# Two products of the delta rule in one of 128 columns, and the query products moved behind the solves

## The chip, the cores and the metric

The kernel runs on one core of a Trainium2 chip. The metric is the device time of one execution in microseconds (us), median of several. The engines are named as the profile names them: PE is the matrix engine (PEld its weight loads), DVE the vector engine, ACT the scalar engine, POOL the GpSimd engine, SP the engine that issues DMAs.

## What is computed

The program is a decoder of two layers over 4 batches of 512 tokens with 128 channels. Each layer has an attention, a cross attention and a feed forward part, with a layer norm after each. The change lies in the attention of the second layer, a delta rule with 16 heads of 64 channels. Cut to what matters, it is:

```python
Q = (x @ Wq).reshape(B, T, H, D)
K = (x @ Wk).reshape(B, T, H, D)
V = (x @ Wv).reshape(B, T, H, D)
beta = jax.nn.sigmoid(x @ Wbeta + b_beta)
K = K / jnp.maximum(jnp.linalg.norm(K, axis=-1, keepdims=True), EPS)
def step(W, inp):
    q_t, k_t, v_t, b_t = inp
    pred = jnp.einsum('bhij,bhj->bhi', W, k_t)
    err = v_t - pred
    W_new = W + b_t[..., None, None] * jnp.einsum('bhi,bhj->bhij', err, k_t)
    o_t = jnp.einsum('bhij,bhj->bhi', W_new, q_t)
    return (W_new, o_t)
W0 = jnp.zeros((B, H, D, D), dtype=x.dtype)
_, O = lax.scan(step, W0, xs)
out = jnp.moveaxis(O, 0, 1).reshape(B, T, H * D)
return out @ Wout
```

## The kernel before

The recurrence is not run token by token. The 512 tokens of a batch are cut into 8 chunks of 64, and 4 heads of one batch make a unit, so that there are 16 units (`u`; `m = u // 2` counts pairs of units, `j = u % 2` the half in the pair). Per unit two things are done.

The preparation, `d_prep_tensor`, `d_prep_scalar` and `d_prep_vector`, works on all chunks of a unit at once. It makes the values (`values`), the queries (`queries`), finishes a block inverse (`corner`, `fold`), multiplies it into the values and keys side by side (`solve`, four times, the result copied by ACT to `d_UW`), and multiplies keys with queries (`products`); DVE masks these into `d_PT`. From `d_UW` four products follow, all fp32 with a 64x64 operand: the transitions (`"da"`, 24 matmuls of 64 columns, `d_UW` times keys), the steps (`"db"`, 28), the reads (`"dr"`, 28, `d_UW` times `d_PT`) and the outputs (`"do"`, 32). DVE turns the transitions into `d_AT` (`d_id` minus the product, line 2001, four instructions) and subtracts the reads from the queries in `d_QT` (line 2013, two instructions). ACT copies the steps to `d_S` and the outputs to `d_OT`.

The chain, `d_chain_tensor` and `d_chain_vector`, runs over the chunks in order: for chunks 1 to 7 a product of `d_S` with `d_AT`, one of `d_S` with `d_QT`, and on DVE an addition to `d_S` (line 2065). After chunk 3 and after chunk 7 DVE adds the finished half to `d_OT` (line 2070). PE then waits for `d_ot`, the second of these additions, and multiplies `d_OT` with the output weights (`d_wo`, 8 matmuls).

`d_order` weaves, per `u`, the chain of unit `u` with the preparation of unit `u + 1`, and with more: in odd `u` up to 9 `d_rows_*` makes the keys of a later pair (its DVE part scales them at line 1675, after a row of small instructions on `d_z`, `d_za`, `d_zb`, `d_zy`, `d_sb` and `d_f`); in even `u` from 2 to 10 `d_turn_*` transposes them (line 1598), multiplies each chunk with itself from `d_KT`, and DVE masks that into `d_L` (line 1687). At the end, from `u` = 13 on, the cross attention (`e_*`) and the start of the feed forward part (`f_*`) are woven in. Each engine runs its instructions in the order in which the woven generators issue them; every `yield` is a place where another generator may be served, and the numbers beside a generator are its share.

Products of these stages take turns in a ring of 5 PSUM banks, `ringD`: whoever takes a bank first waits until its last content has been read, by the semaphore and value that were given when it was taken.

In this stage PE works on quarters of the array. `TILES` sets the order of the matmuls so that four in a row use four different quarters; `solve` takes two of the quarters in turn. One fp32 matmul shows in the trace as two loads and two matmul records.

```python
TILES = [(p, c, half, par) for p in range(2) for c in range(4) for half, par in ((0, 0), (1, 1), (0, 1), (1, 0))]
```

## Time and profile before

| | |
|---|---|
| median of three runs | 1605.43 us (1594.52, 1605.43, 1605.57) |
| the profiled execution | 1597.89 us |
| its span | 1596.1 us |
| PE busy | 1451.0 us, 91% of the span |
| DVE busy | 1125.7 us, 71% |
| ACT busy | 925.6 us, 58% |
| the delta rule's woven stage | from about 1000 to about 1440 us of the span |

The profile gives for every engine what it did and when, how long it sat idle, and what released it. The chain of work that ended last is followed back from the last instruction, each step to what released it. "issue" is time in which an engine waited for nothing that the profile shows.

### The profile page before, as it was taken

The page shows a single profiled execution, that of the slowest core. Times are in us where ns is not written, and L with a number is a line of the kernel's source. Part 1 is how long each engine was busy: PE and PEld are TensorE (multiplying, and loading weights), DVE is VectorE, ACT ScalarE, POOL GpSimd, SP SyncE. Part 2 cuts the span into 40 slices and gives each one's busy share as a digit, 9 for nine tenths or more (in the row PEclk, how much of TensorE's full clock was granted, in tenths as well). Part 3 has the DMA queues.
Part 4 walks back from the last instruction along what each step waited for, and adds up shares of the span by engine and source line. Part 5 has one row for each costly group of instructions (what it writes and reads, how often), then busy time and mean ns, then how long its engine had stood idle before and what let it go on. Part 6 is the DMA issues. An engine that isn't in the chain of part 4 may idle for free.

```text
span 1596.1 us, 44182 instructions
## 1 busy us (share of the span) xinstructions
PE 1451.0 (91%) x19224; PEld 800.5 (50%) x19224; DVE 1125.7 (71%) x2297; ACT 925.6 (58%) x1301; POOL 694.8 (44%) x741
## 2 busy tenths in 40 slices
PE   8888888899999999999988988999999989999996
PEld 4222222343434334333434544787877778775453
DVE  6778877888877885867727668576777765574654
ACT  2788775787867876887672443555455544342220
POOL 2111131566655665676580108457776567010000
PEclk9999999999999999999999999999999999989898
DMA  4000003333322341332302000000000002000000
GB/s 166 1 1 1 1 1 108 106 95 91 95 77 77 91 109 52 104 91 78 94 6 79 1 1 14 16 17 17 4 17 17 17 3 67 28 2 1 8 7 14
DMA packets 32417, 70.80 MB, mean 44 GB/s; under 512 B 5328, under 2 KB 7056, under 8 KB 31968
## 3 DMA queue, kind: packets, MB, share of 16 engines
q1 hardware_dynamic: 32224, 67.98, 14.5%
q8 instruction: 151, 2.47, 0.7%
q14 instruction: 42, 0.34, 0.1%
HBM read 47.45 MB, written 20.51 MB: 43 GB/s over the span
## 4 chain that ended last, share of the span: by engine, by line
PE 62%; ACT 14%; DVE 14%; issue 7%; POOL 2%; DMA 0%; ACTq 0%; DVEq 0%; SPq 0%; POOLq 0%
PE ps L160 60%; ACT b_X L961 3%; ACT a_E L470 3%; DVE b_mx L899 2%; ACT b_EH L169 2%; POOL b_EL L979 1%; DVE a_MX L433 1%; PE ps L242 1%; ACT b_Hk L169 1%; PE ps L1598 1%; DVE b_Lk L840 1%; ACT b_OT L169 1%; DVE X L234 1%; DVE st L172 1%; DVE b_rd L1072 1%
## 5 line engine op out<-in xcount | busy, mean ns | idle before, releaser
L979 POOL TENSOR_TENSOR b_EL<-b_X,b_EH 128x1024 f16<-128x1024 f32 x160 | 341.1, 2132 | 193.5 <-ACT b_EH L169 193.3
L961 ACT ACTIVATE b_X<-ps 128x1024 f32<-128x1024 f32 x160 | 163.7, 1023 | 88.6 <-PE ps L160 86.8
L1784 POOL TENSOR_TENSOR d_tmp<-d_G,d_XI 128x31 f32<-128x31 f32 (+15 forms) x248 | 126.5, 510 | 162.6 <-DVE d_G L1713 143.7
L433 DVE TENSOR_REDUCE a_MX<-ps 128x2 f16<-128x1024 f32 x128 | 155.3, 1227 | 45.7 <-PE ps L160 45.3
L169 ACT ACTIVATE b_EH<-b_X 128x1024 f16<-128x1024 f32 x160 | 169.1, 1057 | 26.0 <-PE ps L160 14.8
L899 DVE TENSOR_REDUCE b_mx<-ps 128x2 f32<-128x1024 f32 x128 | 155.9, 1218 | 37.0 <-PE ps L160 35.1
L160 PE MATMUL ps<-b_M,b_S 128*64 128x512 f16 (+1 forms) x1408 | 175.6, 381 | 3.4 <-ACT b_X L961 3.3
L470 ACT ACTIVATE a_E<-ps 128x1024 f32<-128x1024 f32 x128 | 131.1, 1024 | 49.2 <-PE ps L160 49.0
L1787 POOL TENSOR_TENSOR d_XI<-d_XI,d_tmp 128x31 f32<-128x31 f32 (+15 forms) x248 | 139.6, 563 | 19.4
L160 PEld LDWEIGHTS ps<-b_M,b_S 128*64 128x64 f16 (+1 forms) x1408 | 70.9, 108 | 80.3 <-ACT b_X L961 14.1
L452 POOL TENSOR_TENSOR a_QS<-a_QS,a_MR 128x512 f16<-128x512 f16 x16 | 18.5, 1156 | 201.0 <-ACT a_MR L169 197.1
L2526 POOL TENSOR_TENSOR f_Y<-X,f_bo 128x512 f32<-128x512 f32 x4 | 6.0, 1496 | 188.8 <-DVE X L234 106.9
L160 PE MATMUL ps<-f_XM,f_Wh 128*128 128x512 f16 x256 | 78.2, 388 | 0.0
L160 PE MATMUL ps<-b_Hk,b_Hq 64*128 64x154 f16 (+1 forms) x512 | 66.8, 309 | 12.4 <-DVE b_mx L899 9.9
L160 PE MATMUL ps<-a_E,a_VA 128*32 128x512 f32 x512 | 69.5, 615 | 1.4
L160 PE MATMUL ps<-b_EH,b_VH 128*64 128x512 f16 x320 | 64.7, 400 | 4.2 <-ACT b_OT L169 2.1
L160 PEld LDWEIGHTS ps<-b_Hk,b_Hq 64*128 64x128 f16 x512 | 19.8, 93 | 95.2 <-issue 48.1
L160 PE MATMUL ps<-d_KV,d_XE 64*64 64x128 f32 x1024 | 65.4, 273 | 0.5 <-ACT d_XE L169 0.3
L169 ACT ACTIVATE d_UW<-ps 128x512 f32<-128x512 f32 x64 | 38.2, 597 | 46.3 <-PE ps L160 46.3
L1389 ACT ACTIVATE c_SG<-ps 128x512 f32<-128x512 f32 x36 | 21.5, 597 | 74.1 <-PE ps L160 70.7
L160 PE MATMUL ps<-a_QS,a_KS 32*128 32x512 f16 x256 | 50.0, 387 | 14.8 <-ACT a_E L470 14.3
L2065 DVE TENSOR_TENSOR d_S<-d_S,ps 128x128 f32<-128x128 f32 x96 | 26.9, 280 | 49.5 <-PE ps L160 48.9
(323 smaller groups left out, 3322.3 us busy)
## 6 DMA issues: line engine op xcount, KB each, us to landing
b_S<-s_xk SPq DMA_DIRECT2D x48, 336.0 KB, 6.3
b_M<-s_xq SPq DMA_DIRECT2D x48, 256.0 KB, 5.0
s_xk<-b_Hk SPq DMA_DIRECT2D x16, 336.0 KB, 2.2
s_xk<-b_Lk SPq DMA_DIRECT2D x16, 336.0 KB, 2.5
s_xq<-b_Hq SPq DMA_DIRECT2D x16, 256.0 KB, 2.0
s_xq<-b_Lq SPq DMA_DIRECT2D x16, 256.0 KB, 2.0
d_XI<-eye SPq DMA_DIRECT2D x8, 512.0 KB, 3.8
f_w<-f_w SPq DMA_DIRECT2D x1, 2048.0 KB, 8.7
```

The lines of the kernel that those rows point to most:

```text
L160: return e.matmul(out, lhsT, rhs, start=start, stop=stop, skip_group_check=True)
L169: return e.activation(out, a, ACT.Copy)
L433: v.e.tensor_reduce(out, PS[:, bk:bk + 2, :], AX, ALU.max).then_inc(sem("a_mx"), 1)
L452: p.e.tensor_tensor(a_QS[G % 4], a_QS[G % 4], a_MR[G % 2], ALU.add).then_inc(sem("a_q2"), 1)
L470: a.e.activation(a_E[c][:, 2 * hp:2 * hp + 2, :], PS[:, bk:bk + 2, :], ACT.Exp, scale=float(D) ** -0.5).then_inc(sem("a_ex"), 1)
L899: last = v.e.tensor_reduce(b_mx[:, 0, :, n], PS[:, bk:bk + 2, :], AX, ALU.max)
L961: a.e.activation(b_X[k % 2], PS[:, bk:bk + 2, :], ACT.Exp, scale=0.125).then_inc(sem("b_ex"), 1)
L979: last = p.e.tensor_tensor(b_EL[k % 6], b_X[k % 2], b_EH[k % 6], ALU.subtract)
L1389: a.e.activation(c_SG[n % 3], PS[:, bank["cgu", b, p], :], ACT.Silu).then_inc(sem("c_sl"), 1)
L1784: e.tensor_tensor(tm, a, x, ALU.mult).then_inc(*p.step())
L1787: last = e.tensor_tensor(z, z, tm, ALU.subtract)
L2065: e.tensor_tensor(s, s, PS[:, 6, o:o + 128], ALU.add).then_inc(sem("d_s"), 1)
```

## The change

The masked query products no longer have a tile `d_PT` of their own. DVE writes them over the values, in the half of `d_KV` that lies beside the keys, once the four solves of the unit have read the values (`d_um`). The transitions and the reads then have the same stationary operand `d_UW` and moving operands that lie side by side, so a new function `spread` makes them as one product: per half of the unit (`p`) 12 matmuls of 128 columns and 2 of 64. DVE takes the results apart with eight instructions instead of six, `d_AT` and `d_QT` in turn. The query products move on PE from ahead of the solves to behind them, and the steps come ahead of `spread`. The core of the diff:

```diff
-            def transitions(r, p, c, par):
-                return U[r, at_chunk(p, c, par), 64:128], keys_of(r, p, c, par)
-
-            def reads(r, p, c, par):
-                i = at_chunk(p, c, par)
-                return U[r, i, 64:128], P[r, i, :]
+            def spread(p):
+
+                bk = [ringD.take(t, ("dr", u, p, half), 1, "d_qq", 4 * u + 2 * p + half + 1) for half in range(2)]
+                t.wait_ge("d_u", 4 * u + 4)
+                t.wait_ge("d_pt", 2 * u + 2)
+                for k, c, half, par in TILES:
+                    if k == p and 2 * c + half > 0:
+                        r, n = HALF[half], 2 if 2 * c + half < 7 else 1
+                        last = mm(e, PS[HALF[par], bk[half], 128 * c:128 * c + 64 * n], U[r, at_chunk(p, c, par), 64:128],
+                                  KV[r, c, 0:n, 4 * j + head(p, par), :])
+                last.then_inc(sem("d_rm"), 1)
...
-            products()
             yield
             for k in range(4):
                 solve(k)
                 yield
-            yield
-            update("da", "d_a", "d_am", 64, 128, 1, 6, transitions)
+            products()
             yield
             update("db", "d_b", "d_bm", 64, 128, 0, 6, steps)
             yield
-            yield
-            t.wait_ge("d_pt", 2 * u + 2)
-            update("dr", "d_qq", "d_rm", 256, 64, 1, 7, reads)
+            for p in range(2):
+                spread(p)
+                yield
             yield
             update("do", "d_o", "d_om", 256, 64, 0, 7, outputs)
...
             v.wait_ge("d_ptm", u + 1)
+            v.wait_ge("d_um", 4 * u + 4)
             for par in range(2):
-                e.tensor_tensor(d_PT[:, 8 * par:8 * par + 8, :], PS[:, bank["dp", u, par], :].rearrange("p (i n) -> p i n", i=8),
-                                d_mu.unsqueeze(1).broadcast_to([128, 8, 64]), ALU.mult).then_inc(sem("d_pt"), 1)
-                yield
...
+                e.tensor_tensor(KV[:, :, 0, 4 * j + par:4 * j + 4:2, :].rearrange("p c a n -> p a c n"),
+                                PS[:, bank["dp", u, par], :].rearrange("p (a c n) -> p a c n", a=2, c=4),
+                                d_mu.unsqueeze(1).unsqueeze(1).broadcast_to([128, 2, 4, 64]), ALU.mult).then_inc(sem("d_pt"), 1)
+                yield
+            A = d_AT[j].rearrange("p (c k) a n -> p c k a n", k=2)
             q = d_QT[j].rearrange("p a (c k n) -> p a c k n", c=4, k=2)
+            for p in range(2):
+                v.wait_ge("d_rm", 2 * u + p + 1)
+                for half in range(2):
+                    o = 1 - half
+                    ps = PS[:, bank["dr", u, p, half], :].rearrange("p (c k n) -> p c k n", c=4, k=2)
+                    e.tensor_tensor(A[:, o:o + 3, half, p, :], d_id.unsqueeze(1).broadcast_to([128, 3, 64]), ps[:, o:o + 3, 1],
+                                    ALU.subtract).then_inc(sem("d_a"), 1)
+                    x = q[:, p, o:4, half, :]
+                    e.tensor_tensor(x, x, ps[:, o:4, 0], ALU.subtract).then_inc(sem("d_qq"), 1)
+                yield
...
-                    streams.append((later(9, split(lane)), 18))
+                    streams.append((later(13, split(lane)), 22))
```

PE in a loop with an odd `u` (the preparation of a unit whose keys lie in `d_KV_192`), from the middle of the solves to the outputs, before:

```order
L160 MATMUL ps<-d_KV_192,d_XE 64x128 x16
L160 MATMUL ps<-d_S_217,d_AT_201 64x64 x4
L160 MATMUL ps<-d_QT_211,d_S_217 64x64 x4
L160 MATMUL ps<-d_KV_192,d_XE 64x128 x8
L160 MATMUL ps<-d_S_217,d_AT_201 64x64 x4
L160 MATMUL ps<-d_QT_211,d_S_217 64x64 x4
L160 MATMUL ps<-d_KV_192,d_UW 64x64 x24
L160 MATMUL ps<-d_UW,d_KV_192 64x64 x28
L160 MATMUL ps<-d_QT_211,d_S_217 64x64 x4
L160 MATMUL ps<-d_PT,d_UW 64x64 x60
```

The solves are the rows with `d_XE`, the chain the rows with `d_S`; `d_KV_192,d_UW` are the 24 transitions, `d_UW,d_KV_192` the 28 steps, `d_PT,d_UW` the 28 reads and the 32 outputs. The same place after the change:

```order
L160 MATMUL ps<-d_KV_192,d_XE 64x128 x8
L160 MATMUL ps<-d_QT_210,d_KT_194 64x64 x32
L160 MATMUL ps<-d_S_217,d_AT_201 64x64 x4
L160 MATMUL ps<-d_QT_211,d_S_217 64x64 x4
L160 MATMUL ps<-d_UW,d_KV_192 64x64 x28
L160 MATMUL ps<-d_KV_192,d_UW 64x128 x11
L160 MATMUL ps<-d_KV_192,d_UW 64x64
L160 MATMUL ps<-d_KV_192,d_UW 64x128
L160 MATMUL ps<-d_KV_192,d_UW 64x64
L160 MATMUL ps<-d_QT_211,d_S_217 64x64 x4
```

The query products (`d_QT,d_KT`) now stand behind the last solve, the steps are the first to need `d_UW`, and `spread` has the chain's last product between its two halves; the other half and the outputs follow.

DVE in the same kind of loop, from the last small steps ahead of the key scaling to the second addition to `d_OT`, before:

```order
L2065 TENSOR_TENSOR d_S_217<-d_S_217,ps 128x128
L1668 TENSOR_TENSOR d_sb<-d_z,d_zy 128x32
L1670 TENSOR_TENSOR d_f<-d_zy,d_sb 128x32
L2001 TENSOR_TENSOR d_AT_200<-d_id,ps 128x3x64 x4
L1675 TENSOR_TENSOR d_KV_192<-d_KV_192,d_f 128x512
L2070 TENSOR_TENSOR d_OT_219<-d_OT_219,ps 128x2x256
L1675 TENSOR_TENSOR d_KV_192<-d_KV_192,d_f 128x512 x2
L2013 TENSOR_TENSOR d_QT_210<-d_QT_210,ps 128x2x3x64
L2013 TENSOR_TENSOR d_QT_210<-d_QT_210,ps 128x8x64
```

And after the change, up to the same addition:

```order
L1668 TENSOR_TENSOR d_sb<-d_z,d_zy 128x32
L1670 TENSOR_TENSOR d_f<-d_zy,d_sb 128x32
L2002 TENSOR_TENSOR d_AT_200<-d_id,ps 128x3x64
L2005 TENSOR_TENSOR d_QT_210<-d_QT_210,ps 128x3x64
L2002 TENSOR_TENSOR d_AT_200<-d_id,ps 128x3x64
L2005 TENSOR_TENSOR d_QT_210<-d_QT_210,ps 128x4x64
L1675 TENSOR_TENSOR d_KV_192<-d_KV_192,d_f 128x512
L2002 TENSOR_TENSOR d_AT_200<-d_id,ps 128x3x64
L2005 TENSOR_TENSOR d_QT_210<-d_QT_210,ps 128x3x64
L2002 TENSOR_TENSOR d_AT_200<-d_id,ps 128x3x64
L2005 TENSOR_TENSOR d_QT_210<-d_QT_210,ps 128x4x64
L2063 TENSOR_TENSOR d_OT_219<-d_OT_219,ps 128x2x256
```

The addition to `d_OT`, for which the output product on PE waits, stood ahead of both subtractions from `d_QT`; it now stands behind all eight instructions that take `spread` apart, in this loop and in every other one.

## Rows read from the trace of the kernel before

**Rows 1.** The page: span; busy time and instructions; the queue of instruction transfers (packets, MB).

```profile
span 1596.1 us, 44182 instructions
...
PE 1451.0 (91%) x19224; PEld 800.5 (50%) x19224; DVE 1125.7 (71%) x2297; ACT 925.6 (58%) x1301; POOL 694.8 (44%) x741
...
q8 instruction: 151, 2.47, 0.7%
```

**Rows 2.** Windows: stretch, its length, then busy us (instructions) of PE, PEld, DVE, ACT, POOL; granted clock.

```profile
1117.05:1132.93 15.88, 14.25 (x572) 13.21 (x571) 13.79 (x32) 7.40 (x13) 14.23 (x22) 1.00 0.02 4
1137.59:1159.14 21.55, 18.75 (x717) 17.11 (x717) 13.40 (x40) 10.35 (x17) 10.89 (x24) 1.00 0.02 4
```

**Rows 3.** Chain that ended last, 1116 to 1160 us: start, us, what.

```profile
1126.85 0.61 ACT d_UW L169
...
1131.14 1.29 issue
...
1157.01 1.56 issue
...
1159.14 0.59 PE ps L242 x4
```

**Rows 4.** Timeline of PEld from 1126 us, loop u = 3: start, us, instructions, [idle before].

```profile
1126.53 0.37 PEld L160 LDWEIGHTS ps<-d_S,d_AT 64*64 64x64 f32 x8
...
1127.56 0.83 PEld L160 LDWEIGHTS ps<-d_KV,d_UW 64*64 64x64 f32 x48 [0.43 <-issue]
1128.26 1.05 PEld L160 LDWEIGHTS ps<-d_UW,d_KV 64*64 64x64 f32 x55
...
1129.46 1.53 PEld L160 LDWEIGHTS ps<-d_PT,d_UW 64*64 64x64 f32 x93
1132.42 0.44 PEld L160 LDWEIGHTS ps<-d_PT,d_UW 64*64 64x64 f32 x24 [1.43 <-issue]
1132.93 1.19 PEld L160 LDWEIGHTS ps<-d_wo,d_OT 128*128 128x128 f32 x10
```

**Rows 5.** Timeline of PEld from 1145 us, loop u = 4: last solve, first `d_KT` product.

```profile
1146.24 0.85 PEld L160 LDWEIGHTS ps<-d_KV,d_XE 64*64 64x64 f32 x16
...
1149.65 1.05 PEld L160 LDWEIGHTS ps<-d_KT 64*64 64x64 f32 x64 [1.09 <-ACT d_UW L169]
```

**Rows 6.** DMA from 1118 to 1158 us, 40 slices of 1 us: GB/s by packet start; totals.

```profile
GB/s 16 0 0 0 16 0 0 16 0 0 0 16 0 0 0 16 0 0 0 0 0 16 0 0 16 0 0 0 16 0 0 0 0 0 16 0 0 16 0 0
DMA packets 10, 0.16 MB, mean 4 GB/s; under 512 B 0, under 2 KB 0, under 8 KB 0
```

**Rows 7.** Timeline 1078 to 1108 us: loads for 32 and for 128 columns.

```profile
1087.54 1.09 PEld L160 LDWEIGHTS ps<-d_XE,d_L 32*32 32x32 f32 x64 [0.21 <-issue]
...
1093.98 1.73 PEld L160 LDWEIGHTS ps<-d_KV,d_XE 64*64 64x64 f32 x32
```

**Rows 8.** Timeline of DVE from 1120 us, loop u = 3.

```profile
1122.46 0.69 DVE L1990 TENSOR_TENSOR d_PT<-ps,d_mu 128x512 f32<-128x512 f32 x1
...
1126.86 0.66 DVE L172 SCALAR_TENSOR_TENSOR d_zy<-d_zb,d_zy 128x64 f32<-128x64 f32 x1
...
1127.63 0.60 DVE L1668 TENSOR_TENSOR d_sb<-d_z,d_zy 128x32 f32<-128x32 f32 x1
...
1128.58 1.15 DVE L2001 TENSOR_TENSOR d_AT<-d_id,ps 128x192 f32<-128x192 f32 x4
1129.64 0.68 DVE L1675 TENSOR_TENSOR d_KV<-d_KV,d_f 128x512 f32<-128x512 f32 x1
1130.25 0.68 DVE L2070 TENSOR_TENSOR d_OT<-d_OT,ps 128x512 f32<-128x512 f32 x1
...
1132.58 1.14 DVE L2013 TENSOR_TENSOR d_QT<-d_QT,ps 128x384 f32<-128x384 f32 x2
```

**Rows 9.** DVE groups by shape from 1000 to 1480 us: the mask into `d_L`.

```profile
L1687 DVE TENSOR_TENSOR d_L<-ps,d_ml 128x512 f32<-128x512 f32 x26 | 16.7, 684 | 24.5 <-PE ps L160 24.5
```

**Rows 10.** Chain that ended last, 1412 to 1427 us, shares by line.

```profile
by line: DVE f_XM L2468 30.8%; PE ps L160 21.8%; DVE f_Wl L172 16.1%; DVE X L234 6.9%; DVE e_Qp L2300 5.0%; DVE st L172 4.6%; issue 4.2%; ACT f_mk L169 4.1%; DVE d_AT L2001 3.6%; DVE d_S L2065 2.7%; DVE st L181 1.2%; DVE st L187 1.2%; DVE s
```

More of the change, by code:

```diff
@@ L1797, in d_prep_tensor @@
             KV, KT, L, X = d_KV[m % 3], d_KT[m % 2], d_L[m % 2], d_XE[u % 2]
-            Q, P, U, x = d_QT[j], d_PT, d_UW, d_XS[b % 2]
+            Q, U, x = d_QT[j], d_UW, d_XS[b % 2]
             def values(k):
@@ L1944, in d_prep_scalar @@
                 yield
-            yield
-            yield
             a.wait_ge("d_bm", u + 1)
@@ L1992, in d_prep_vector @@
                 yield
-            for _ in range(4):
-                yield
-            v.wait_ge("d_am", u + 1)
-            A = d_AT[j].rearrange("p (c k) a n -> p c k (a n)", k=2)
-            for half in range(2):
-                o = 1 - half
-                ps = PS[:, bank["da", u, half], 128 * o:128 * o + 384]
-                for a in range(2):
-                    last = e.tensor_tensor(A[:, o:o + 3, half, 64 * a:64 * a + 64], d_id.unsqueeze(1).broadcast_to([128, 3, 64]),
-                                           ps.rearrange("p (c a n) -> p c a n", c=3, a=2)[:, :, a], ALU.subtract)
-                last.then_inc(sem("d_a"), 1)
@@ L2004, in d_prep_vector @@
-            yield
-            yield
-            yield
-            v.wait_ge("d_rm", u + 1)
-            q = d_QT[j].rearrange("p a (c k n) -> p a c k n", c=4, k=2)
-            for half in range(2):
-                o = 1 - half
-                x = q[:, :, o:4, half, :]
-                ps = PS[:, bank["dr", u, half], :].rearrange("p (a c n) -> p a c n", a=2, c=4)
-                e.tensor_tensor(x, x, ps[:, :, o:4], ALU.subtract).then_inc(sem("d_qq"), 1)
-            yield
-            yield
+            A = d_AT[j].rearrange("p (c k) a n -> p c k a n", k=2)
@@ L2019, in d_chain_tensor @@
+            for _ in range(3):
+                yield
         def d_chain_tensor(t, u):
```

14 lines of the change are left out of this document (6 added, 8 removed).

## Prediction

> **What bounds the kernel now.** I read the page first: PE is busy 1451 of 1596.1 us [rows 1]. Then the windows of two loops of the stage. In the one that scales keys (u = 3) PE is busy 14.25 of 15.88 us, but DVE is busy 13.79 as well; in the one that transposes keys (u = 4) PE has 18.75 of 21.55 us and DVE 13.40 [rows 2]. So PE sets the pace in both, and in the first DVE is only just behind it. What PE loses between its instructions stands in the chain of work that ended last, over the same two loops [rows 3]. There are three kinds of loss:
>
> - It waits for the last copy to `d_UW` before the transitions. The last solve ends at 1126.53 and the chain's two products then take 0.47 us; the transitions start at 1127.56 [rows 4]. About 0.6 us, with the copy itself in the chain.
> - It waits with nothing to wait for, "issue": 1.29 us at 1131.14 and 1.56 us at 1157.01 [rows 3], each inside the long row of small products with `d_PT` [rows 4].
> - In the transposing loops it waits 1.09 us for the copies ahead of the first `d_KT` product [rows 5].
>
> The "issue" waits are the arrival of PE's own instructions, as I read the DMA rows. Queue q8 moves 151 packets, 2.47 MB; PE and PEld together have 38,448 instructions [rows 1], so 64 bytes each and about 255 to a packet. In the dense stretch the packets start 3 to 4 us apart: slices 0, 4, 7, 11, 15 and again 21, 24, 28 [rows 6]. The window of u = 3 holds 1143 instructions in 15.88 us, 4.5 packets; that of u = 4 holds 1434, 5.6 packets in 21.55 us [rows 2]. Both give 3.5 to 3.85 us for a packet. A row of small products uses one up in 128 x 15 ns = 1.9 us, and then runs dry.
>
> **The change, part by part.** The reference time is the profiled execution, 1597.89 us, span 1596.1; the median of three is 1605.43. I make the sum against the mean of all four, 1600.9 us, since one execution lies 11 us below the others.
>
> *The product itself.* A matmul of 64 columns shows as two loads. 48 of them take 0.70 us from the first to the start of the next group [rows 4], so a matmul costs 0.029 us; transitions and reads cost 52 x 0.029 = 1.52 us. The trace has no 128 columns over four quarters. It has them over two: 32 loads in 1.73 us, 0.054 us each, 0.108 per matmul [rows 7]. Bounds for one of the 24 new matmuls are 0.029 (the columns cost nothing) and 0.108 us (four quarters help no more than two). I take half the upper one, 0.054, because the solves' price is that of streaming columns and four quarters share it twice as far. That gives 24 x 0.054 + 4 x 0.029 = 1.41 us, a gain of 0.1 us per unit. The bounds give a gain of 0.7 and a loss of 1.2 us.
>
> The row of 32-column products weighs in here: 64 loads in 1.09 us [rows 7], 16 ns each, no cheaper than 64 columns at 15 ns. The Trainium skill (TensorEngine Tiling (Array Packing), Instruction Overhead) says that a matmul has some 60 cycles of overhead, so that one column costs as much as 60; the trace agrees that narrower is no cheaper, though 15 ns at 2.4 GHz is 36 cycles. By that rule 128 columns cost twice 64, and the merge would give PE nothing; the sum would be 16 x 0.1 = 1.6 us less.
>
> *Instructions.* 24 matmuls fewer are 96 instructions, 0.375 packet: 1.4 us per unit, wherever the packets set the pace.
>
> *Query products behind the solves.* Their 32 matmuls, 64 x 15 ns = 1.0 us, are only moved. They now cover the last copy to `d_UW`, 0.6 us, and in the five transposing loops they stand between transposes and the first `d_KT` product and cover its 1.09 us.
>
> *The masks.* Before, the masks ran under the solves and nobody waited. Now the first `spread` needs both. I count from the end of the last solve, with the times of [rows 4, 8]. In a loop with key rows (odd u, 1 to 9): the query products end at 1.05. DVE: mask 1.25 to 1.9, a `d_zy` step 0.66, second mask to 3.2. PE has had chain and steps since 2.4 and waits 0.8. `spread` runs to 4.0. DVE meanwhile adds `d_S`, and makes `d_sb` and `d_f`, until 4.3. Then four instructions that take the first half apart: `d_AT` costs 1.15 / 4 = 0.29 and `d_QT` 1.14 us for both, so 0.29 + 0.29 + 0.29 + 0.36 = 1.2 us, to 5.5. A key scaling of 0.7, to 6.2; the second half, to 7.4; and only then the addition to `d_OT`, 0.6, to 8.0.
>
> *What is late next.* The output product on PE waits for that addition. Before, it was over at 1130.93 and the output product started at 1132.93 [rows 4, 8], 2 us later, 6.4 us after the last solve. Now PE is through with the outputs at about 5.2 (halves of `spread`, a bank released by the first `d_QT`, outputs 1.0 us) and stands until 8.0. Behind the waiting output product stand the next unit's values and queries, and so DVE and ACT. Taking off the 1.05 us of query products that moved in here, it is 6.95 us against 6.4: a loss of 0.55 us, in five loops 2.8 us. The "issue" wait and the copy wait are gone, but the wait for `d_OT` is as long as both and more.
>
> *Transposing loops* (even u, 2 to 10). Before, 1147.1 to 1159.14 us, 12.0 us, of which 1.09, 1.56 and about 0.6 us are waits [rows 3, 5], so 8.8 us of work. After, 8.8 + 1.0 - 0.1 = 9.7 us to the end of the outputs, the first half of `spread` ending 2 us earlier, at 7.8. The masks are long done. DVE: first half to 9.0, then two masks into `d_L`, 1.4 us [rows 9], which now stand between the halves, to 10.5; second half to 11.7; `d_OT` at 12.4. Less 1.0 is 11.4, against 12.0, or 12.6 where a transpose of `X` stands ahead. I take a gain of 0.9, in five loops 4.5 us.
>
> *Loops without either* (u = 0, 11, 12, 13). Masks at 2.6, first half of `spread` to 3.4, DVE to 4.7, 5.9, `d_OT` at 6.5; less 1.05 is 5.5 against 6.4. Gain 0.9, in four 3.6 us; I take 3.2, since the last two are mixed with other work.
>
> *Last preparation* (u = 14). Here DVE is on the chain itself, with `f_XM` at 30.8% and `f_Wl` at 16.1% [rows 10]. Both masks now stand behind these and `spread` waits for them, two more instructions are added, and `e_Qp` stands behind the first half. A loss of 0.5 to 2.5, I take 1.5 us. Moving `f_Wl` back by four steps makes this no worse.
>
> *The first unit* has free room; 0.3 us for the covered copy.
>
> Sum: -2.8 + 4.5 + 3.2 - 1.5 + 0.3 = 3.7, so 4 us. 1600.9 - 4 = 1597 us.
>
> **The rivals.**
>
> *The packets still decide, and the wait for `d_OT` is hidden.* If DVE runs well ahead and its addition comes by the end of the outputs, each unit is worth what its instructions are: 1.3 us in eight loops, 2.0 in five transposing ones (96 instructions, and the 1.09 us in part), 20 us, less 1.5: 1582 us. For it: packets 3 to 4 us apart. Against it: DVE has 13.79 of 15.88 us in one kind of loop [rows 2], and its order is fixed, addition last. Chance 0.28, 1573 to 1588.
>
> *Everything goes at once*, the refill waits with it, and 30 us are won: 1571 us and below. It needs DVE to be no bound at all. Chance 0.04.
>
> *Slower: the addition to `d_OT` comes later than I count.* One mechanism, DVE's tail in front of the output product. If each of its eight pieces costs 0.12 us more, because a piece of 192 elements does not overlap the one before as the four in a row did, the tail grows by 1 us in 15 units: 4 - 15 = -11, 1612 us. It decides from 0.27 us per unit on, the 4 us spread over 15 units; so a small error of mine turns the sign. Chance 0.22, 1601 to 1620.
>
> *As forecast*, 1588 to 1601: 0.46.
>
> **How the numbers follow.** A measurement of this kernel can tell about 1% from no change, 16 us. Faster by more: 0.04, and two thirds of 0.28, with a little of the middle case, 0.24. Slower by more: the top third of 0.22, 0.08. Within: 0.68. The range 1580 to 1612 leaves out the fastest case, the faster third of the packet case and the top of the slower one, 0.04 + 0.10 + 0.05. The likeliest case alone has 1588 to 1601.
>
> **What the profile after would show.** PE waits ahead of the output product for DVE's `d_OT`, 1 to 3 us in nearly every unit: if this row is missing, my main step is wrong and the time is near 1582. A new wait of PE for the mask in `d_KV`, 0.3 to 0.8 us, in loops without transposes. The waits for `d_UW` ahead of the steps are gone, and the 1.09 us in front of `d_KT` products. "issue" waits above 0.5 us are fewer than one per unit. Loads with 128 columns are 27 ns apart (54 would mean that four quarters share nothing). q8 has 6 packets fewer, 145. The forecast fails if the eight pieces on DVE cost other than 1.2 us per half, or if the spacing of packets is not a limit but follows from PE's pace.

## The result, and the profile after

| | before | after |
|---|---|---|
| median | 1605.43 us (1594.52 to 1608.83, 5 runs) | 1652.38 us (1642.87 to 1655.02, 5 runs) |
| profiled execution | 1597.89 us, span 1596.1 | 1642.87 us, span 1640.7 |
| PE busy | 1451.0 us, 91% | 1456.9 us, 89% |
| start of the output product in loop u = 0, and in u = 15 | 1057.5, 1471.8 | 1062.1, 1518.9 |

The change is 2.85% slower: ratio 1.0285, 95% interval 1.0246 to 1.0324. I had forecast 1597 us, range 1580 to 1612; the time lies 40 us above the range. The page of the changed kernel, against [rows 1]:

```profile
PE 1456.9 (89%) x18456; PEld 808.8 (49%) x18456; DVE 1126.7 (69%) x2329; ACT 926.8 (56%) x1301; POOL 695.6 (42%) x741
...
q8 instruction: 145, 2.38, 0.6%
```

PE has 768 matmul records fewer and six instruction packets fewer, as the diff says, and yet stands idle longer. The place is certain: between the output products of u = 0 and u = 15 lie 414.3 us before and 456.8 after, 42.5 of the 44.6 us by which the spans differ. By kind of loop: the five that transpose keys (u = 2 to 10, even) are 25.6 us longer, the five that scale keys (odd u to 9) 9.5, the last five 7.4. Every kind lost, where I had expected a gain in the transposing loops and in most of the last ones. The output product of u = 0 itself starts 4.6 us later, although the last group ahead of the stage starts 2.0 us earlier (997.87 against 999.82 us): another 6.6 us are lost in the first preparation and loop u = 0. Of the kernels below, those that have only the query products moved, or moved as in the change, lose 6 to 8 us there, those with the products ahead of the solves at most 2, so this is the move's. (`three` and `four`, where `queries` is moved as well, lose 2 to 4.) After the last output product the changed kernel is 2.4 us shorter, which no edit explains.

Part of the loss goes with PE's clock. The trace shows it granted in full (2.4 GHz) or at half (1.2 GHz). Between the output products of u = 0 and u = 15 it is at half for 13.7 us before and for 30.7 us after, most of the latter in u = 2, 6, 8 and 13, where the kernel before has none. From execution to execution the time follows it as well: over 94 executions of the kernel before, the mean granted clock lies between 0.972 and 0.986, and the time falls by 1.4 us for each 0.001 more. The five executions of the changed kernel have a mean of 0.974, those before 0.979; by that slope, and this is an estimate, some 8 of the 47 us go with the lower clock. No run changes the clock alone, so whether it falls because PE waits more is not shown.

PE's waits in the changed kernel, from 1000 to 1520 us (who waits, for what; us in total, times, longest):

```profile
PE ps L160 <- DVE d_L L1687: 10.1, 5, 2.4
PE ps L160 <- ACT d_KT L169: 9.6, 5, 2.3
PE ps L160 <- DVE d_OT L2063: 8.4, 8, 1.8
PE ps L160 <- issue: 8.2, 13, 0.9
PE ps L1598 <- ACT d_UW L169: 6.4, 5, 1.3
PE ps L242 <- DVE X L234: 6.4, 4, 2.3
PE ps L160 <- DVE d_KV L1991: 5.4, 8, 2.8
PE ps L160 <- ACT d_XE L169: 5.2, 6, 1.4
```

The same view of the kernel before, for PE:

```profile
PE ps L160 <- issue: 20.0, 19, 1.8
PE ps L160 <- ACT d_KT L169: 4.4, 5, 0.9
PE ps L160 <- ACT d_UW L169: 4.3, 10, 1.1
```

The 20 us without a releaser have fallen to 8, and further than the row says: eight of its 13 waits, 0.71 us each, stand ahead of the first solve of a unit and end 0.1 us after ACT's copy to `d_XE`. They belong to that copy, which makes its row 10.9 us and leaves 2.5 us of waits for instructions. But six waits for other engines are new and the one for `d_KT` has doubled, and only two of them (for `d_OT` and for the mask in `d_KV`) are in my prediction. Those for `d_L`, for `d_KT` and for `d_UW` ahead of the transposes belong to loops that transpose. This is one of them, u = 4, PEld first, then ACT and DVE (start, us, instructions, idle before and releaser; where a row of PEld says "issue", the list above names the releaser of PE's wait):

```profile
1160.94 0.71 PEld L160 LDWEIGHTS ps<-d_KV,d_XE 64*64 64x64 f32 x12
...
1162.85 1.02 PEld L160 LDWEIGHTS ps<-d_QT,d_KT 64*64 64x64 f32 x64 [0.17 <-issue]
1165.30 0.42 PEld L1598 LDWEIGHTS ps<-ident,d_KV 128*128 128x128 f32 x4 [1.42 <-ACT d_UW L169]
...
1170.79 1.05 PEld L160 LDWEIGHTS ps<-d_KT 64*64 64x64 f32 x64 [1.76 <-issue]
...
1174.82 1.81 PEld L160 LDWEIGHTS ps<-d_KV,d_UW 64*64 64x64 f32 x92 [1.98 <-issue]
1178.82 0.42 PEld L242 LDWEIGHTS ps<-ident,X 128*128 128x128 f32 x4 [2.19 <-issue]
1179.21 0.97 PEld L160 LDWEIGHTS ps<-d_wo,d_OT 128*128 128x128 f32 x8
```

```profile
1164.16 0.60 ACT L169 ACTIVATE d_KT<-ps 128x512 f32<-128x512 f32 x1 [2.97 <-PE ps L160]
1164.65 0.59 ACT L169 ACTIVATE d_UW<-ps 128x512 f32<-128x512 f32 x1
...
1169.21 0.98 ACT L169 ACTIVATE d_S<-ps 128x512 f32<-128x512 f32 x2 [2.62 <-PE ps L160]
1170.08 0.60 ACT L169 ACTIVATE d_KT<-ps 128x512 f32<-128x512 f32 x1
```

```profile
1173.62 0.41 DVE L2005 TENSOR_TENSOR d_QT<-d_QT,ps 128x256 f32<-128x256 f32 x1
...
1174.02 1.28 DVE L1687 TENSOR_TENSOR d_L<-ps,d_ml 128x512 f32<-128x512 f32 x2
```

ACT's first copy to `d_KT` may only run when the query products of this unit have read the tile it overwrites (`d_ptm`, in `d_turn_scalar`). Before, those products stood ahead of the solves and were long through. Now they start at 1162.85, behind two groups of transposes; ACT stands 2.97 us, and its fourth copy to `d_UW`, whose product was ready, stands behind it. PE's third group of transposes needs the ring bank which that copy frees, and waits 1.42 us. Next, the last `d_KT` copy stands on ACT behind the two to `d_S`: 1.76 us. Then the second half of `spread` needs banks that hold the `d_L` products, and DVE masks these only after it has taken the first half apart: 1.98 us. Last, the transposes of `X` wait for DVE's line 234, which stands behind the second half and the addition to `d_OT`: 2.19 us.

In loops that scale keys the picture is that of the prediction, and one wait more. Loop u = 3, PEld, then DVE:

```profile
1135.62 0.88 PEld L160 LDWEIGHTS ps<-d_KV,d_XE 64*64 64x64 f32 x16 [0.87 <-issue]
...
1139.17 0.88 PEld L160 LDWEIGHTS ps<-d_KV,d_XE 64*64 64x64 f32 x16
...
1142.85 0.77 PEld L160 LDWEIGHTS ps<-d_KV,d_UW 64*64 64x64 f32 x26 [0.40 <-DVE d_KV L1991]
...
1147.49 1.64 PEld L160 LDWEIGHTS ps<-d_wo,d_OT 128*128 128x128 f32 x14 [1.80 <-DVE d_OT L2063]
```

```profile
1143.91 0.35 DVE L2002 TENSOR_TENSOR d_AT<-d_id,ps 128x192 f32<-128x192 f32 x1 [0.34 <-PE ps L160]
...
1144.71 0.41 DVE L2005 TENSOR_TENSOR d_QT<-d_QT,ps 128x256 f32<-128x256 f32 x1
...
1146.77 0.68 DVE L2063 TENSOR_TENSOR d_OT<-d_OT,ps 128x512 f32<-128x512 f32 x1
```

The wait of 0.87 us ahead of the first solve is the one I had missed. `fold` is copied by ACT to the block inverse (`d_mt`, the releaser `d_XE` of the list above), and the query products used to stand between `fold` and the first solve and cover that copy.

### The profile page after: what moved, and what is told of

Its sections match the earlier page's. It is cut to its first block, busy times and chain, and to the rows that moved or that the text cites. A ratio compares the mean times of both kernels' runs of the same rounds, so it can differ in the third digit from the quotient of the medians.

```text
span 1640.7 us, 42711 instructions
## 1 busy us (share of the span) xinstructions
PE 1456.9 (89%) x18456; PEld 808.8 (49%) x18456; DVE 1126.7 (69%) x2329; ACT 926.8 (56%) x1301; POOL 695.6 (42%) x741
## 4 chain that ended last, share of the span: by engine, by line
PE 60%; DVE 17%; ACT 15%; issue 6%; POOL 1%; DMA 0%; ACTq 0%; DVEq 0%; SPq 0%; POOLq 0%
PE ps L160 57%; ACT b_X L961 3%; ACT a_E L470 3%; DVE b_mx L899 2%; ACT b_EH L169 1%; POOL b_EL L979 1%; DVE a_MX L433 1%; PE ps L242 1%; ACT b_Hk L169 1%; DVE d_QT L2005 1%; DVE X L234 1%; PE ps L1598 1%; DVE d_AT L2002 1%; DVE b_Lk L840 1%; DVE d_KV L1991 1%
## 5 line engine op out<-in xcount | busy, mean ns | idle before, releaser
L169 ACT ACTIVATE b_EH<-b_X 128x1024 f16<-128x1024 f32 x160 | 169.1, 1057 | 25.9 <-PE ps L160 14.7
L160 PE MATMUL ps<-d_KV,d_XE 64*64 64x128 f32 x1024 | 69.4, 281 | 10.9 <-issue 5.7
L160 PE MATMUL ps<-b_Hk,b_Hq 64*128 64x154 f16 (+1 forms) x512 | 66.8, 309 | 12.9 <-DVE b_mx L899 10.4
L2058 DVE TENSOR_TENSOR d_S<-d_S,ps 128x128 f32<-128x128 f32 x96 | 27.0, 281 | 66.8 <-PE ps L160 66.3
L160 PE MATMUL ps<-d_KV,d_UW 64*64 64x64 f32 (+1 forms) x1920 | 55.7, 263 | 18.1 <-DVE d_L L1687 10.1
L160 PEld LDWEIGHTS ps<-d_KV,d_XE 64*64 64x64 f32 x1024 | 59.8, 140 | 13.8 <-issue 13.8
```

Source lines behind the costliest of these rows:

```text
L160: return e.matmul(out, lhsT, rhs, start=start, stop=stop, skip_group_check=True)
L169: return e.activation(out, a, ACT.Copy)
L2058: e.tensor_tensor(s, s, PS[:, 6, o:o + 128], ALU.add).then_inc(sem("d_s"), 1)
```

## The experiments

Ratios are against the kernel before on the same chip, with the 95% interval. The kernel before has medians of 1601.5 to 1605.4 us on the chips used, so a difference in us between two kernels that did not run on the same chip is uncertain by some 4 us, and by more where the intervals are wide. The theories: **order**, that the query products lost the work they covered and put ACT's queue out of step; **tail**, that DVE's eight pieces stand in front of what PE needs (`d_OT`, banks); **packets**, that fewer PE instructions are worth 1.3 us per unit.

**The two parts apart.** First the move without the merge, and the merged product without the move, its masks one by one behind the solves that free them:

```diff
 # move_alone, against the kernel before (units 0 to 13)
-            products()
             yield
             for k in range(4):
                 solve(k)
                 yield
+            products()
...
 # merge_alone, against the changed kernel (units 0 to 13)
+            products()
             yield
             for k in range(4):
                 solve(k)
                 yield
-            products()
...
-            v.wait_ge("d_um", 4 * u + 4)
             for par in range(2):
+                v.wait_ge("d_um", 4 * u + 2 * par + 2)
```

> The kernel before, with the query products behind the four solves in units 0 to 13 (units 14 and 15 as before), the masks into d_PT four steps later on DVE; transitions, reads and their take-apart unchanged. Order theory (the place of the query products carries the loss of 47 us): the waits of the changed kernel come back without the merge. About 0.95 us ahead of the first solve for ACT's copy d_mt, 12 us in all, and 3 to 5 us in each of the five transposing loops, because the copies to d_KT stand on ACT behind a wait for the query products; I expect 1605 + 30 = 1635 us, 1622 to 1650. Tail theory (DVE's eight pieces and the addition to d_OT behind them carry it): the move alone only covers waits, 1605 or a little less, 1592 to 1608. My prediction's count for the move was a gain of 10 us.

Measured: 1633.93 us, 1.0196 (1.0116 to 1.0276). The move alone costs 32 us, where the change has 47, and the order theory's two waits show in it, that of the transposes and the missed one ahead of the first solve. They are not all of it: "issue" is 33.1 us here, against 20.0 before, 5.7 of it ahead of the first solves as above. The other 27.4 are waits for instructions inside rows of small products, 7 us more than before; the moved products now stand in one row with the steps and transitions. And the mean granted clock is 0.974.

```profile
PE ps L160 <- issue: 33.1, 31, 2.1
PE ps L1598 <- ACT d_UW L169: 6.4, 5, 1.3
PE ps L160 <- ACT d_XE L169: 5.2, 6, 1.4
```

> The changed kernel, with the query products back ahead of the solves in units 0 to 13 and each mask on DVE placed behind the two solves that read its half of the values (d_um at 4u + 2 and 4u + 4); spread and the eight pieces on DVE stay. Order theory: the waits ahead of the first solve (12.6 us in the changed kernel) and most of those in the transposing loops go; left are the tail and the d_UW wait; 1652 - 35 = 1617 us, 1605 to 1628. Tail theory: most of the loss stays, 1640 to 1655, since the addition to d_OT still stands behind the eight pieces.

Measured: 1654.58 us, 1.0313 (1.0235 to 1.0391). A miss, and the price I gave to the order theory was wrong here. PE's waits say why this kernel isn't the clean half that I took it for:

```profile
PE ps L160 <- ACT d_KT L169: 14.0, 10, 2.3
PE ps L160 <- DVE d_S L2067: 11.4, 22, 1.7
PE ps L160 <- DVE d_L L1687: 10.1, 5, 2.4
PE ps L160 <- DVE d_OT L2072: 9.2, 9, 1.8
```

The wait for `d_XE` is gone, but DVE now stands in its queue at masks that wait for solves, and the chain's additions to `d_S` behind them are late 22 times. The waits for `d_L` and `d_OT` are those of the changed kernel, so they come with the merge.

So a cleaner one: query products ahead of the solves and masked into `d_PT` just as before, and a `spread` whose moving operand is one access pattern from the keys across to `d_PT`, two rows of 64 words a fixed distance apart.

```diff
+                        if 2 * c + half < 7:
+                            k0 = KV_AT[m % 3] + 1024 * c + 512 + 64 * (4 * j + head(p, par))
+                            k1 = 35492 - 9508 + 64 * i
+                            x = d_both[r, k0:k0 + 64]
+                            x = bass.AP(x.tensor, x.offset, [list(x.ap[0]), [k1 - k0, 2], [1, 64]])
+                            last = mm(e, PS[HALF[par], bk[half], 128 * c:128 * c + 128], U[r, i, 64:128], x)
```

> The merge without anything else: the kernel before, with transitions and reads as one product of 128 columns (spread, two halves, eight pieces on DVE), but the query products stay ahead of the solves and are masked into d_PT as before, under the solves. The moving operand is one access pattern that reaches from the keys to d_PT. Sum theory: the loss of the whole change (47 to 51 us) is that of the move (32 us, measured) and that of the merge, so the merge costs 15 to 19 us: 1618 us (1612 to 1624), with waits for d_L, 10 us, and d_OT, 9 us, in the trace and PE's issue waits down from 20 to under 10 us. Rival, my prediction's: the merge is worth the 96 instructions of a unit, 1.3 us in 13 loops, less the tail: 1590 to 1603. Second rival: the time of the kernel with the masks per parity (1654.6) is the merge's own and not that of its masks: 1640 to 1655.

Measured: 1635.92 us, 1.0191 (1.0134 to 1.0247). The merge by itself costs 33 us, twice the sum theory's price, in none of the three forecasts' ranges and far from my prediction's gain. Move and merge together make 65 us where the change has 47, so their losses overlap. By kind of loop, in the profiled executions, the overlap is 5 us in the transposing loops (9.1 and 21.8 us alone, 25.6 together) and 11 in those that scale keys (11.2 and 9.7 alone, 9.5 together). One part shows: the 27.4 us of waits for instructions that the move has alone are 2.5 us in the changed kernel. The rest was not tried. PE's waits in this kernel:

```profile
PE ps L160 <- ACT d_KT L169: 15.5, 12, 2.3
PE ps L160 <- DVE d_L L1690: 10.2, 5, 2.4
PE ps L160 <- DVE d_OT L2071: 9.8, 9, 2.1
PE ps L160 <- issue: 8.2, 10, 1.5
```

**Repairs of order in the changed kernel.** Each takes one of the waits away and leaves the work as it is.

```diff
 # turn_later
-                    streams.append((later(18, turn(lane, m)), 30.59))
+                    streams.append((later(21, turn(lane, m)), 33.59))
...
 # ot_first: steps between the two halves of the take-apart, not behind them
                 yield
-            for _ in range(3):
-                yield
+                if p == 0:
+                    for _ in range(2):
+                        yield
```

> The changed kernel, with the transposes of the keys and what follows them three steps later in the five transposing loops, so that PE has issued the query products before the first transpose and ACT's copy to d_UW no longer stands behind a copy to d_KT that waits for them. The five loops are 25.7 us longer than before in the changed kernel. Order theory: the waits of 1.3 to 1.6 us behind the fourth d_UW copy in five loops go, and the second d_KT product no longer waits for a copy behind the two of d_S: 7 to 15 us less, 1642 us (1636 to 1647). Tail theory: the masks into d_L only come later, in front of the addition to d_OT; no gain or 5 us worse, 1650 to 1658.

Measured: 1641.36 us, 1.0245 (1.0168 to 1.0323), 11 us less by the medians, 6 by the ratios, whose intervals overlap with the changed kernel's. The profiled executions are clearer: the five transposing loops are 12.9 us longer than before instead of 25.6; the other kinds change by 1.5 us or less.

> The changed kernel, with two more steps between the two halves of the take-apart on DVE, so that in the loops where it fits (10 of 16) the second addition to d_OT stands between the halves and no longer behind all eight pieces. Tail theory, step 'what is late next' of my prediction: PE's wait ahead of the output product falls by the 1.2 us of a half in ten loops, 8 to 12 us less, 1642 us. Order theory: the waits that the trace shows for d_OT are 10.7 us over eight loops, of which some comes back as a wait of the next chain for d_AT and d_QT: 2 to 8 us less, 1647 us. If the tail carried most of the loss, over 20 us would have to go.

Measured: 1638.99 us, 1.022 (1.0143 to 1.0296), 13 us less by the medians, 10 by the ratios. That is the tail theory's number, and more than I gave it by the waits. But it isn't most of the loss.

> The changed kernel with two of the three repairs of order: transposes three steps later, addition to d_OT between the halves; the queries' products stay where the change has them. Against the kernel with three repairs (1610.0) it prices the cover of ACT's copy d_mt ahead of the first solve. By the waits of the changed kernel 12.6 us are to be had there, and a product of 512 columns that leaves its place behind the corner uncovers the copy d_NW (14.0 us of gaps in 13 loops in the kernel with three): expected 1652 - 11 - 13 = 1628 us, that is 18 us above the three. If the two waits only change places, 1610 to 1615.

Measured: 1625.86 us, 1.0131 (1.0102 to 1.0159). 26 us less, clear of the noise; the two add up within the error.

```diff
 # three: with both of the above
-            queries(0)
             yield
             values(1)
...
             corner()
             yield
-            queries(1)
+            queries(0)
             yield
             fold()
             yield
+            queries(1)
             yield
             for k in range(4):
```

> The changed kernel with three repairs of order at once: the transposes three steps later (gave 11 us alone), the addition to d_OT between the halves (13 us alone), and the second queries' product moved from ahead of fold to behind it, with the first one ahead of fold, so that a product of 512 columns stands between fold and the first solve and covers ACT's copy d_mt (waits of 12.6 us in 13 loops). Order theory: the three add up, 1652 - 11 - 13 - 9 = 1619 us (1612 to 1626), and the 0.95 us ahead of the first solve are gone. Rival: PE's clock or DVE's order takes back what is won in one place, no better than the best single one, 1638.

Measured: 1609.97 us, 1.0048 (1.0021 to 1.0075). Between `turn_ot` and this lie 16 us by the medians and 13 by the ratios: the price of the cover that the query products had given to ACT's copy of `fold`, less what the moved queries uncover in turn. The largest wait that is left in it, and the place, loop u = 4:

```profile
PE ps L1598 <- ACT d_KT L169: 9.1, 5, 2.2
```

```profile
1158.92 0.42 PEld L1598 LDWEIGHTS ps<-ident,d_KV 128*128 128x128 f32 x4 [1.70 <-ACT d_KT L169]
```

```profile
1157.40 0.98 ACT L169 ACTIVATE d_S<-ps 128x512 f32<-128x512 f32 x2 [2.63 <-PE ps L160]
1158.26 0.61 ACT L169 ACTIVATE d_KT<-ps 128x512 f32<-128x512 f32 x1
```

The copies to `d_S` block ACT from about 1154.8 to 1158.3, and the third copy to `d_KT`, ready at 1155.2, is behind them. One step less ahead of them, one more behind:

```diff
 # four: in d_prep_scalar
                 yield
+            yield
             a.wait_ge("d_bm", u + 1)
...
-            for _ in range(3):
+            for _ in range(2):
                 yield
```

> The kernel with three repairs, and in addition ACT's two copies to d_S one step later, behind all four copies to d_KT instead of between the second and the third. In the kernel with three, PE waits 1.70 us in each of five transposing loops for the third copy to d_KT (9.1 us), which stands on ACT behind the copies to d_S. Order theory: 5 x 1.5 = 7 to 8 us less, 1602 us (1598 to 1606). Rival: the next product waits for something else at once (a bank behind d_L, the clock): 1608 to 1611.

Measured: 1602.69 us, 0.999 (0.9966 to 1.0015). 7.3 us less (9 by the ratios), and the wait of 9.1 us is gone from the list. Four changes of order and none of the work have brought the changed kernel back to the time before. In the profiled executions the stretch from the output product of u = 0 to that of u = 15 says the same, by how much it is longer than before: 42.5 us in the changed kernel, 32.1 in `turn_later`, 32.0 in `ot_first`, 18.4 in `turn_ot`, 9.4 in `three`, 0.9 in `four`.

**The same repairs on the clean merge.** `beside_ot` is `beside` with the steps between the halves; `beside_four` adds the later copies to `d_S`, `beside_five` the later transposes.

> As the kernel beside, with the two halves of the take-apart on DVE two steps further apart, so that the second addition to d_OT falls between them. In the changed kernel the same step gave 13 us of 51. Expected by the tail theory: 8 to 12 us under the kernel beside. If the waits for d_L in the transposing loops are what the merge costs, only 3 to 5 us under it.

Measured: 1618.99 us, 1.0106 (1.0076 to 1.0136), 17 us less; the tail weighs more here than I gave it.

> The kernel beside_ot (the merge alone, products ahead of the solves, masks into d_PT, addition to d_OT between the halves, 1619.0) with ACT's copies to d_S one step later, behind all four copies to d_KT. PE's gaps there: 10.8 us in five loops for the last copy to d_KT, 12.3 us in six for a bank behind the masks into d_L. Expected 5 x 1.7 = 8 us less, 1611; if the wait for d_L ends last anyway, 1617 to 1619.

Measured: 1606.09 us, 1.001 (0.9985 to 1.0036), 13 us less, also more than expected.

> As beside_four, and the transposes of the keys three steps later as well, so that DVE's first pair of masks into d_L is through before the second half of spread takes their banks. Expected: both gaps of the transposing loops go (12.3 and 10.8 us), less 2 us for what then waits: 1619 - 19 = 1600 us (1595 to 1606), beside or under the kernel before. If the merge is worth nothing even without those waits, it stays above 1606.

Measured: 1600.3 us, 0.9986 (0.996 to 1.0012). All of the 33 us is back, and not a microsecond beyond it that the measurement can tell. So against the kernel before, order accounts for the whole loss. But where is the gain of 96 instructions per unit?

**What the merged instruction is worth.** Each matmul of 128 columns as two of 64, with the same banks, order and take-apart, first in the changed kernel (`halves`), then in `beside_five` (`five_halves`):

```diff
 # halves, against the changed kernel; five_halves splits its own operand in the same way
-                        last = mm(e, PS[HALF[par], bk[half], 128 * c:128 * c + 64 * n], U[r, at_chunk(p, c, par), 64:128],
-                                  KV[r, c, 0:n, 4 * j + head(p, par), :])
+                        for i in range(n):
+                            last = mm(e, PS[HALF[par], bk[half], 128 * c + 64 * i:128 * c + 64 * i + 64], U[r, at_chunk(p, c, par), 64:128],
+                                      KV[r, c, i, 4 * j + head(p, par), :])
```

> The changed kernel with each matmul of 128 columns in spread issued as two of 64 columns side by side: same banks, same order, same take-apart, 88 matmul records and loads more per unit. It prices the merged instruction by itself. If instructions set PE's pace (a packet of 16 KB in 3.5 to 3.85 us, 1.3 us per unit) the time rises by up to 16 x 1.3 = 20 us, to 1672. If the waits for DVE and ACT decide, PE has room: 0 to 6 us more, 1652 to 1658, and the issue waits come back in rows that now show waits for DVE. I expect the second, 1656.

Measured: 1663.2 us, 1.0371 (1.0314 to 1.0428), 11 us more (14 by the ratios), between the two forecasts. PE's waits without a releaser rise from 8.2 to 13.8 us with it.

> The kernel beside_five (1600.3) with each matmul of 128 columns issued as two of 64. In the changed kernel this cost 11 us. Here the waits for ACT and DVE in the transposing loops are gone, so if instruction packets set the pace in the small products, the 96 instructions of a unit must now cost their full 1.3 to 1.4 us: 1600 + 16 x 1.35 = 1621 us (1615 to 1625). If what the merge saves is only PE's own time (48 matmuls x 0.029 us against 24 x 0.051, 0.17 us per unit), it costs 3 us: 1603.

Measured: 1600.95 us, 0.9979 (0.995 to 1.0008). The packet theory asked for 21 us and got 0.6 against `beside_five`; against `five_b` (below, nearly the same kernel), which ran on the same chip, it is 1.7 us. Both are within the error, some 4 us: 21 us is excluded, the 3 us of the second forecast are not. With 151 packets again, PE's waits without a releaser go up from 6.9 to 11.5 us in the profiled executions; the whole does not move by an amount that can be told, for the waits for `d_OT` and for `X` fall by about as much (2.9 to 0.3 and 2.8 to nothing). Why the same split cost 11 us in the changed kernel, where more is late, stays open. The second row is of `five_halves`:

```profile
PE ps L160 <- issue: 6.9, 10, 1.2
```

```profile
PE ps L160 <- issue: 11.5, 13, 1.8
```

**Whose gain is a repair?** The kernel before with the later transposes, nothing else:

> The kernel before with the transposes of the keys three steps later and nothing else. It asks whether the repair of order that gave 5.7 us between beside_four and beside_five belongs to the merge or would have helped anyway. The kernel before shows 6.2 us of gaps between transposes and the first product of d_KT in five loops, 2 of which could go: theory that the gain is the merge's alone (masks into d_L between the halves of spread): 1602 to 1608. Rival, that it helps any kernel of this shape: 1595 to 1599.

Measured: 1593.39 us, 0.9949 (0.9917 to 0.998). The rival holds: the repair is not the merge's. Part of what `beside_five` won back was to be had without the merge. On the same chip ran `five_b` (`beside_five`, with the halves left together in units 14 and 15):

> The kernel beside_five with the two halves of the take-apart apart by two steps only for units below 14, and adjacent for units 14 and 15, where the step set e_Qp and others between them and PE waits 3.2 us for the bank of the first half. Expected 1 to 3 us less than 1600.3; within the error of the measurement if the wait for d_QT at that place is passed on to the next.

Measured: 1599.21 us, 0.9991 (0.996 to 1.0022); no difference from `beside_five` that can be told, and 5.8 us above `before_turn`. Both ran once more, side by side on another chip:

> The kernel before with the transposes three steps later, once more, side by side with five_b_again on one chip, to compare the merge with and without on the same order of the transposes. First measured at 0.9949 [0.9917, 0.998] of before: expected 1594 us, 0.993 to 0.997.

Measured: 1592.59 us, 0.9926 (0.99 to 0.9952). This is the fastest kernel here, 0.7% below the one before, after 0.5% at the first measurement.

> The merge with masks into d_PT and all repairs of order (five_b, first 1599.2 us, 0.9991 of before), beside turn_again. Waits inside PE's rows of like products are 11 us fewer than in the kernel with the repair and without the merge (10.1 against 21.4 us), yet the stage is as long. If the merge is worth nothing, 1597 to 1600 and no faster than turn_again; if it is worth the 11 us, 1583 to 1590.

Measured: 1600.27 us, 0.998 (0.9957 to 1.0004). On the same order of transposes, the kernel with the merge is 7.7 us slower than the one without. PE's waits of the two from 1050 to 1475 us, without the merge first:

```profile
PE ps L160 <- issue: 16.0, 16, 1.8
```

```profile
PE ps L160 <- issue: 6.3, 9, 1.2
PE ps L160 <- DVE d_OT L2071: 3.2, 5, 1.0
PE ps L160 <- DVE e_Qp L2301: 3.0, 2, 2.1
PE ps L160 <- ACT d_S L169: 3.0, 5, 0.6
PE ps L242 <- DVE X L234: 2.9, 3, 1.4
```

9.7 us less without a releaser; 12.1 us in four waits for DVE and ACT, of which the other kernel has 0.6. That is where the expected gain went, as far as the waits show it: the time that PE used to spend on waiting for its instructions, it now spends on waiting for results that come later.

## Why the prediction was wrong

Point by point, in its order.

*What bounds the kernel.* That PE sets the pace and stands still in three places was read rightly. That the "issue" waits come with the instruction packets is right: all 19 of them in the kernel before lie a whole number of packets apart (last section), they fell with the change and rose again in both kernels of halves. Their price was not in my sum, but it was my strongest rival, and there it was the error. I took the packet spacing for a rate that each saved instruction would pay back, 1.3 us per unit. In the repaired order the split kernel is 0.6 to 1.7 us slower, for 16 units, within an error of 4.

*The product itself.* I took 0.054 us for a matmul of 128 columns over four quarters. Measured, by the row of u = 3 above: 26 loads in 0.77 us, of which the last takes 0.13, so 25.6 ns from one to the next and 0.051 us per matmul. Right, and worth the 0.1 to 0.2 us per unit of the text. By the rule of the Trainium skill (TensorEngine Tiling (Array Packing), Instruction Overhead), as I applied it, 128 columns cost twice 64 and the merge gives PE nothing. The runs put them at 1.76 times, 0.051 against 0.029, so it was off by little.

*Query products behind the solves: the step that failed.* "Are only moved. They now cover the last copy to `d_UW`", and in the count of each kind of loop the 1.05 us of these products were taken off, since they left the place ahead of the solves. That place did not get shorter. From one output product to the next first solve a transposing loop takes 9.76 us before and 9.73 after, and the five loops that scale keys together 65.3 and 66.3, because PE stands there for ACT's copy of `fold`, which the products had covered: 13 to 16 us (`turn_ot` against `three`). I asked what they would cover at the new place and not what they covered at the old one. And the move set something free later: ACT's first `d_KT` copy waits for `d_ptm`. I had written that these products "cover" the gap in front of the `d_KT` product, but that gap's cause, ACT's queue, now waited for them in turn: 6 to 11 us (`turn_later`). Only gains in the text; a loss of 32 us on the chip (`move_alone`).

*The masks.* Forecast 0.8 us in loops that scale keys; the trace has 0.40 in u = 3. Place right, size half. What I missed is in the first unit, for which I had put down a gain of 0.3 us: 2.8 of the 5.4 us stand there in one wait, at 1026.30, because DVE works on `X` (line 234, four instructions, 2.3 us) between the two masks.

*What is late next.* In the loops that scale keys this was right, mechanism and size: the output product waits for the addition to `d_OT` behind all eight pieces, 1.80 us in u = 3, and a half costs 1.2 us (1143.91 to 1145.12). From the end of the last solve to the output product I had 8.0 us; in u = 3 it is 7.44 (1140.05 to 1147.49), and over the five loops 7.6 on the mean, against 6.1 before. Less the 1.05 us, that is the 0.55 us of the forecast. In the loops without either, 6.5 us was forecast and u = 11 has 6.7; but I set it against the 6.4 us of u = 3, and u = 11 takes 4.85 before, so the gain of 0.9 was a loss of 0.8. `ot_first` won 10 to 13 us with this addition, more than the loss that I had counted for it; in its trace the same stretch is 4.8 us shorter in the loops that scale keys and 3.4 in the transposing ones.

*Transposing loops: the second step that failed.* From the last solve to the output product I forecast 12.4 us; in u = 4 it is 17.56 (1161.65 to 1179.21), on the mean of the five 17.8, against 12.7 before. I had even placed the two masks into `d_L` between the halves, and counted them as DVE's time alone. I did not ask who holds the banks: the second half of `spread` takes those that the masks free, and PE waits 10.1 us in five loops. I had also left ACT out of the count of these loops altogether, where PE waits 9.6 us for `d_KT` and 6.4 for `d_UW`. Forecast 0.9 us less in each; they are 5.1 us longer in each.

*Last preparation.* Forecast 1.5 us more. The stretch that I read for it [rows 10] lies in loop u = 14, and that loop is 0.4 us shorter after the change. The loss stands one loop ahead: u = 13, which I had among the loops that gain, is 5.3 us longer, and takes 20.5 us from the last solve to the output product instead of 14.7.

*The rivals and the range.* None of them had the order of ACT's queue in it, nor a bank that comes free late, nor a lower clock, so the slower one was too short at 1620, and the range with it. Of the signs that I named, most came true (the mask's wait, 145 packets, the loads 26 ns apart, fewer waits without a releaser, no wait ahead of the first `d_KT` product), the wait for `d_OT` in 8 loops of 15 and not in nearly all, and the time was still 55 us off. A list of expected waits shows what one has thought of; it doesn't bound what one hasn't.

What stays open: the single waits do not add up to the measured differences exactly (`ot_first` gave more than the wait for `d_OT` shows), and the lower clock may be a part of what they lack; why the losses of move and merge overlap in the loops that scale keys; why the split instruction cost 11 us in one order and nothing that can be told in another; and how much of the last 7.7 us of the merge is DVE's and how much ACT's.

## What to carry to other kernels

When work is moved, make two lists: what waits at its new place that it now covers, and what waited at its old place and was covered by it; then follow every semaphore that the moved work gives, on each in-order queue, to what stands behind the instruction that waits for it. When a ring of banks is shared, a consumer's instruction that moves behind another one delays every later taker of its bank, on another engine and for another product. And what fewer instructions are worth depends on the order of everything else: issuing the merged instruction in two parts prices it, and here the price was 11 us in one order and nothing that could be told in the other. So measure it in the order that is to stay. Last, give a repair to the old kernel as well before the new one is credited with it.

## What the runs showed of the hardware

PE's waits for instructions fall at the borders of packets. Counted along PE's matmul records, the 19 "issue" waits of the kernel before (20.0 us) lie 127, 255, 510, 637 or 765 records apart, give or take one: whole multiples of 127.5, and with a load for each record that is the 255 instructions of a packet. So such a wait can be told from one whose releaser the profile has missed: of the eight of 0.71 us in the changed kernel, seven lie 25 records or more off that grid.

Most of the scatter between executions of one kernel goes with PE's granted clock: over 94 executions of the kernel before, 1590 to 1614 us, time and mean granted clock have a correlation of -0.93.

A moving operand whose two rows of 64 words lie thousands of words apart, in `d_PT` and among the keys, costs nothing extra on PE: in `beside_five` 24 loads of the merged product take 0.72 us from the first to the end of the last, as long as in the changed kernel's transposing loop, where the two rows are neighbours. So two operands need not be copied side by side to be multiplied as one. Here is `beside_five`, then the changed kernel:

```profile
1131.39 0.72 PEld L160 LDWEIGHTS ps<-d_KV,d_UW 64*64 64x64 f32 x24
```

```profile
1171.72 0.72 PEld L160 LDWEIGHTS ps<-d_KV,d_UW 64*64 64x64 f32 x24
```

And three places in the order of one group of transposes were worth 0.5 to 0.7% in the kernel before; with the merge on top and the order repaired for it, the kernel was 0.5% slower than with that repair alone.
